# First gated layer on the column layout: 128-byte load runs, the second factor turned, the following norm beside its output

## The reference, cut to what matters

```python
# L0_conv, z = _ln_c(x); i and j are the two positions, c the channel
zn = _layernorm(z, ln_in_w, ln_in_b)
a = sigmoid(zn @ Wga + bga) * (zn @ Wla + bla)
b = sigmoid(zn @ Wgb + bgb) * (zn @ Wlb + blb)
k = einsum('bimc,bmjc->bijc', a, b)            # the only one that contracts a's second with b's first position
out = sigmoid(zn @ Wgo + bgo) * (_layernorm(k, ln_o_w, ln_o_b) @ Wlo + blo)
x = x + out
# L0_ffn: experts choose their top tokens, from the router's logits over all tokens
t = tokens(x);  t = t + L0_ffn(_ln_t(t), ...)
```

## Time and profile before

| | us |
|---|---|
| median of three runs | 665.69 (665.5 to 666.53) |
| the profiled execution | 664.4 |
| its span | 662.6 |
| PE, DVE, ACT, POOL busy in it | 461.7, 424.8, 286.3, 250.3 |

### The profile page before, as it was taken

One profiled execution on the slowest core, in us unless ns is written; L12 is line 12 of the kernel. 1 busy time (PEld: TensorE's weight loads), 2 busy tenths in 40 slices (PEclk: granted clock), 3 DMA queues, 4 the chain that ended last, 5 costly groups with the idle time before them and its releaser, 6 DMA issues.

```text
span 662.6 us, 8339 instructions
## 1 busy us (share of the span) xinstructions
PE 461.7 (70%) x3015; PEld 358.8 (54%) x3015; DVE 424.8 (64%) x829; ACT 286.3 (43%) x658; POOL 250.3 (38%) x310
## 2 busy tenths in 40 slices
PE   2788744799476774798369983798389736738775
PEld 1457642578243653398349972498256625615443
DVE  6796459533958579601954469501958595499996
ACT  2776535601475455565460015566379544000000
POOL 1893554100467158200050003200359376045563
PEclk9999965876689785899859996989579975559999
DMA  6000000000000000000000000000000000001212
GB/s 203 1 1 1 1 1 0 0 1 0 1 0 1 1 0 2 0 1 1 1 0 1 1 2 1 0 1 1 1 0 1 1 1 0 1 0 29 36 30 35
DMA packets 19576, 6.01 MB, mean 9 GB/s; under 512 B 17068, under 2 KB 19244, under 8 KB 19501
## 3 DMA queue, kind: packets, MB, share of 16 engines
q1 hardware_dynamic: 19534, 5.46, 3.6%
HBM read 3.36 MB, written 2.10 MB: 8 GB/s over the span
## 4 chain that ended last, share of the span: by engine, by line
PE 41%; DVE 35%; POOL 10%; issue 8%; ACT 5%; DMA 1%; DVEq 0%; SPq 0%; POOLq 0%
PE psum L1242 6%; DVE stats L279 5%; POOL z L1513 5%; PE psum L1003 4%; DVE ab L647 4%; PE psum L1002 4%; PE psum L506 4%; PE psum L386 4%; PE psum L536 4%; DVE stats L282 3%; DVE z L292 3%; DVE stats L286 2%; PE psum L1385 2%; PE psum L1024 2%; ACT z_t L318 2%
## 5 line engine op out<-in xcount | busy, mean ns | idle before, releaser
L333 POOL TENSOR_TENSOR z<-z,stats 128x496 f32<-128x496 f32 (+1 forms) x64 | 79.2, 1238 | 177.2 <-DVE stats L289 177.2
L386 PE MATMUL psum<-ident,z 128*128 128x128 f32 x256 | 59.2, 377 | 77.8 <-POOL z L333 75.6
L386 PEld LDWEIGHTS psum<-ident,z 128*128 128x128 f32 x256 | 41.1, 192 | 108.0 <-POOL z L333 74.7
L506 PE MATMUL psum<-wp_L,z_t 64*128 64x320 f32 x384 | 65.9, 482 | 11.9 <-DVE tmp L647 6.4
L309 ACT ACTIVATE squares<-z 128x512 f32<-128x512 f32 x64 | 40.3, 630 | 57.5 <-DVE z L292 57.3
L506 PEld LDWEIGHTS psum<-wp_L,z_t 64*128 64x128 f32 x384 | 37.8, 202 | 35.6 <-issue 29.4
L1513 POOL TENSOR_TENSOR z<-gate 128x512 f32<-128x512 f32 x31 | 39.1, 1282 | 30.1 <-DVE gate L1488 30.1
L1095 ACT ACTIVATE ab<-psum,mv 128x128 f32<-128x128 f32 x112 | 41.1, 367 | 19.5 <-PE psum L1003 9.0
L318 ACT ACTIVATE z_t<-psum 128x512 f32<-128x512 f32 x56 | 39.7, 715 | 21.3 <-PE psum L386 21.1
L1003 PE MATMUL psum<-ab,R_vt 128*128 128x128 f32 x224 | 48.5, 300 | 0.0
L1002 PE MATMUL psum<-z_t,wbnt 128*128 128x128 f32 x224 | 46.4, 291 | 0.8 <-DVE wbnt L1148 0.8
(11 more groups left out here) (243 smaller groups left out, 1029.0 us busy)
## 6 DMA issues: line engine op xcount, KB each, us to landing
x_rows<-in_x_dram SPq DMA_DIRECT2D x4, 512.0 KB, 6.9
out_dram<-x_cols SPq DMA_DIRECT2D x32, 64.0 KB, 1.9
par<-in_par_dram SPq DMA_DIRECT2D x1, 644.5 KB
w<-in_w_dram SPq DMA_DIRECT2D x1, 264.0 KB
w<-in_w_dram SPq DMA_DIRECT2D x1, 256.0 KB
mask<-in_mask_dram SPq DMA_DIRECT2D x1, 64.0 KB
row<-in_row_dram SPq DMA_DIRECT2D x1, 3.3 KB
w2l<-in_w2l_dram SPq DMA_DIRECT2D x1, 2.0 KB
```

The lines of the kernel that those rows point to most:

```text
L333: pool.tensor_tensor(Z4[:, r, :, 0:last_c], Z4[:, r, :, 0:last_c], rstd, ALU.mult).then_inc(L.s["z"], 1)
L386: m = pe.transpose(bank(b % 2)[:, k * N:(k + 1) * N], block_of(Z)(4 * b + k), ident[:, :])
L506: m = pe.matmul(bank(slot_bank(s) + h, 2 * 5 * C), ZT[rows, s, :], wp[l][rows, :, :], start=True, stop=True)
```

## The change

L0 moves to the column layout: its source is `XC` and its scratch `XR`. The load writes `XC` from DRAM with the first position inside the partition, so every descriptor moves 32 channels, 128 bytes. Each quarter is 4 DMAs, one for each g, 16 in all in place of 4; the parameters still come after the first quarter. With the second position on the partitions it is `b` that must be turned (`BT`, same storage, same helper, same number of transposes), and the products come out on columns. V0 is gone. F0 takes its chunks straight from L0's last step (`x_chunks(t0)`), its norm is handed over as `after`, and its first logits product waits until L0 has left the PSUM banks (`banks_free`).

```diff
-        X_LOADED = [[(x_in[q * LOADS // Q], 16)] for q in range(Q)]
+        X_LOADED = [[(x_in[q * LOADS // Q], 16 * G)] for q in range(Q)]
-        t0 = stage("L0", "norm weights ones tri", "at_ps at_act at_dve", src=XR, scratch=XC, eps=0, e2=EPS)
-        v0 = stage("V0", "turn_x", src=XR, dst=XC)
+        t0 = stage("L0", "norm weights ones tri", "bt_ps bt_act bt_dve", src=XC, scratch=XR, eps=0, e2=EPS)
-        v0.ready = x_done(t0)
-        f0.ready = [turned(v0)] * Q
+        f0.ready = x_chunks(t0)
+        f0.banks_free = [(t0.s["o_mul"], t0.at["o_mul"] + S // 4)]
...
-                lhs, rhs = AT, ABt[:, 1]
+                lhs, rhs = BT, ABt[:, 0]
-                    turn_pe(pe, L, b, lambda c: ABt[:, 0, c, :], "at_ps", "at_act", "at_dve")
+                    turn_pe(pe, L, b, lambda c: ABt[:, 1, c, :], "bt_ps", "bt_act", "bt_dve")
...
+                    if b == 0:
+                        wait_all(pe, L.banks_free)
                     pe.wait_ge(L.s["zt"], L.at["zt"] + b + 1)
                     m = pe.matmul(bank(2 + r), gw[:, q, :], ZT[:, 4 * b:4 * b + 4, :], start=(q == 0), stop=(q == 1))
...
-            X4, D4 = blocks(XR), x_d.rearrange("i (g s) c -> i g (s c)", g=G)
+            XC4, D4 = blocks(XC), x_d.rearrange("(g s) j c -> j g s c", g=G)
-                f = slice(q * NC // G // LOADS, (q + 1) * NC // G // LOADS)
-                sp.dma_start(XR[:, :].rearrange("p (g f) -> p g f", g=G)[:, :, f], D4[:, :, f]).then_inc(x_in[q], 16)
+                r = slice(q * S // LOADS, (q + 1) * S // LOADS)
+                for g in range(G):
+                    sp.dma_start(XC4[:, g, r, :], D4[:, g, r, :]).then_inc(x_in[q], 16)
...
-            tri_pool(pool, t0, None)
-            ln_pool(pool, f0)
+            tri_pool(pool, t0, f0)
...
-            tri_act(act, t0, None)
-            turn_x_copy(act, v0, 0)
-            ln_act(act, f0)
+            tri_act(act, t0, f0)
...
-            tri_dve(dve, t0, None, {
+            tri_dve(dve, t0, f0, {
-            turn_x_copy(dve, v0, 1)
-            ln_dve(dve, f0)
...
-            turn_x_pe(pe, v0)
```

More of the change, by code:

```diff
@@ L121, in build @@
         AB = sb("ab", [N, 2 * NC])
-        AT = ZT
+        BT = ZT
         GATE = sb("gate", [N, NC])
@@ L524, in tri_pe @@
             if L is t0:
-                lhs, rhs = AT, ABt[:, 1]
+                lhs, rhs = BT, ABt[:, 0]
                 for b in range(C // 4):
-                    turn_pe(pe, L, b, lambda c: ABt[:, 0, c, :], "at_ps", "at_act", "at_dve")
+                    turn_pe(pe, L, b, lambda c: ABt[:, 1, c, :], "bt_ps", "bt_act", "bt_dve")
             for b in range(C // 4):
                 if L is t0:
-                    pe.wait_ge(L.s["at_dve" if b % 2 else "at_act"], L.at["at_dve" if b % 2 else "at_act"] + b // 2 + 1)
+                    pe.wait_ge(L.s["bt_dve" if b % 2 else "bt_act"], L.at["bt_dve" if b % 2 else "bt_act"] + b // 2 + 1)
                 if b >= 4:
@@ L588, in tri_act @@
                 for b in range(0, C // 4, 2):
-                    turn_copy(act, L, b, AT[:, 4 * b:4 * b + 4, :], "at_act", "at_ps")
+                    turn_copy(act, L, b, BT[:, 4 * b:4 * b + 4, :], "bt_act", "bt_ps")
             warm_table(act, ACT.Sqrt)
@@ L657, in tri_dve @@
                 for b in range(1, C // 4, 2):
-                    turn_copy(dve, L, b, AT[:, 4 * b:4 * b + 4, :], "at_dve", "at_ps")
+                    turn_copy(dve, L, b, BT[:, 4 * b:4 * b + 4, :], "bt_dve", "bt_ps")
             for b in range(1, C // 4, 2):
@@ L1559, in _ @@
             out4 = out_d.rearrange("(g s) j c -> j g s c", g=G)
-            XC4 = blocks(XC)
             for b in range(S // 4):
```

## The result

The changed kernel takes 657.49 us in the median of four runs (655.41 to 660.4); the kernel before, 665.61. The ratio is 0.9878, 95% interval 0.9832 to 0.9924: 8.1 us less, where 7.8 were forecast. A second set of six runs of the unchanged text gave 0.9881 (0.9863 to 0.9900). The profiled execution took 659.11 us, so its span is one of the longer ones, and 5.3 us shorter than the span before.

The account below looks back on a forecast made before the run. A chain of waits shared by PE and DVE was taken as the bound, transfers holding 1%. Seam - 9.0 plus load + 1.2 gave - 7.8, from 665.69 to 657.9 us; own range 656 to 660, over the cases 655.5 to 662.5.

Parts of the forecast that it names:

- The seam: Between L0's output and F0's norm: dropping V0 and interleaving the norm gains 8.6 to 9.4 us, taken as 9.0.
- The turned factor: In L0, turning `b` in place of `a`, with the same transposes, copies and product shapes, costs 0.
- The load: At the start, short-packet quarters and four issues bring the parameters 0.4 to 2.0 us later, taken as 1.2, all on the path.
- The rate: Column load of x: packets of 128 bytes take 9.4 to 12.2 ns per engine, taken from the output store's bursts.
- The sign that I had named: At the start, the load's busy slices should show 200 to 220 GB/s.
- A: L0's norm becomes bound by the load at 16 to 22 ns a packet, losing 2 to 7 us; chance 0.14.
- B: The load, from 24 ns a packet, makes the change lose; 671.9 us at 30 ns; chance 0.06.
- Rival C: Behind F0's norm PE's clock could fall to the lower level, adding 4 us, 661.9 in all; chance 0.08.
- my own sign: The prediction is wrong if the stages behind 120 us are longer than before.
- Rival D: At the seam F0's norm still waits for L0's end, so only the turn goes: 7.1 less 1.2, 659.8 us; chance 0.04.

Follow-up runs that it names:

- Experiment 3: Changed kernel with F0's norm again behind L0 on POOL, ACT and DVE, column layout, load and missing V0 kept; 660.36 us (0.9921).
- experiment 1: The changed kernel run again with no edit, against the kernel before; 657.13 us, all runs 656.5 to 659.6.
- experiment 6: Changed kernel with unread PE transposes of the identity filling idle time in the norms of SC and R2; 657.51 us.
- experiment 2: Changed kernel with load runs of 1 KB, still sixteen DMAs, so the layers compute on the turned image; 655.34 us (0.9848).
- experiment 9: Kernel before, row layout, with its load cut into 16 DMAs with runs of 1 KB; 666.61 us (1.0013).
- experiment 10: Changed kernel with every x load DMA doubled into the gates' buffer, ACT waiting for the copies before the first gate; 665.45 us (0.9987).
- experiment 8: Kernel before with parameters issued ahead of x and DVE's first weight step ahead of the norm's first step; 664.96 us (0.9988).
- experiment 5: Changed kernel with the two parameter loads issued by ACT at its start, beside x's first quarter on the sync queue; 657.37 us (0.9870).

## Why the prediction was right, point by point

*The seam, 9.0 us.* Measured: 9.17 and 9.49 us in two profiles. The analogues told it because the interleaved pipeline is the same code on the same tiles; L3's stretch, 39.47 us, was nearer than L1's, as argued: the changed kernel's two are 39.68 and 39.36. Experiment 3 splits it into the turn (7.3) and the interleaving (1.9). The wait `banks_free` sits where R1's did: PE's first router product begins at 102.02, behind the last L675, as in L1. Behind the last root nothing moved (4.54 us before, 113.09 + 0.60 - 109.15 = 4.54 after).

*The turned factor, 0.* From the first L366 to the first L557 the kernel before took 13.75 us and the changed one 69.47 - 55.72 = 13.75.

*The load, 1.2 us.* In size, the parameters came 0.81 us later in the first profile and 1.09, 1.04 and 1.56 later in the three others with this start (experiments 1, 3 and 6), 1.1 in the mean, all against one profile of the kernel before. In mechanism, I had them wait behind 4096 short packets and behind four issues. Experiments 2 and 9, with an eighth of the packets and the same delay, seem to speak against it. The DMA view settles more: the parameters' packets are the only ones of 2 KB and more at the start, 129 in all, so they can be counted apart, as the total less those under 2 KB. Two of these views, before and after, from 0 to 5.5 us:

```profile
DMA packets 643, 1.12 MB, mean 203 GB/s; under 512 B 16, under 2 KB 528, under 8 KB 643
...
DMA packets 4184, 0.65 MB, mean 118 GB/s; under 512 B 4160, under 2 KB 4160, under 8 KB 4184
```

That is 115 of the 129 before and 24 after. The same count, in steps of 0.25 us:

| | first seen by | most by | all 129 by | DVE's first weights |
|---|---|---|---|---|
| before | 4.00 (4) | 5.50 (115) | 6.50 | 7.01 |
| changed | 4.75 (1) | 6.75 (111) | 7.50 | 7.82 |
| experiment 1 | 5.00 (6) | 7.00 (116) | 7.50 | 8.10 |
| experiment 2, 1 KB | 3.75 (3) | 5.75 (113) | 7.75 | 8.28 |
| experiment 9, 1 KB, rows | 3.75 (3) | 5.75 (113) | 7.50 | 8.05 |

In the changed kernel the parameters start some 0.75 to 1 us later, when x's first quarter is through (3952 short packets by 4.75 us, 4118 by 5.00), inside the 4.4 to 5.1 that I had put down, and end as much later. This is the predicted mechanism. Whether the packets or the issue held them is not separated: their issue begins at 3.27 us, and with the 1.15 us that experiment 2 has from issue (2.60) to first packets (3.75) they could have started at 4.4. In the two forms with runs of 1 KB they start no later than before, and 113 are through by 5.75. But the last 16 take until 7.50 or 7.75, while x's next packets pass between them (344 GB/s in all from 5.75 to 7.75 us in experiment 2); before, 124 were through by 5.75 and the last by 6.50. So the cut into four DMAs a quarter has a delay of its own, of about the same size, which I had not foreseen. Why the last packets lag there, no run shows.

*The rate.* The store's rate, with its gaps, was a good stand-in for the load's. Windows of the changed kernel, GB/s in the last column:

```profile
5.00:10.00 5.00, 1.20 (x5) 1.17 (x6) 4.02 (x12) 0.63 (x1) 0.12 (x1) 1.00 1.00 225
10.00:15.00 5.00, 2.44 (x8) 1.71 (x8) 2.67 (x9) 0.94 (x2) 0.00 (x0) 1.00 1.07 169
```

The second is x alone: 169 GB/s, 12.1 ns a packet for each of 16 engines, between the 9.4 and 12.2 drawn from the store's burst and at its slow end. The sign that I had named, 200 to 220 GB/s, was too high: it left the gaps out. It is about half of the 344 GB/s of the 1 KB runs; whether the run length or the pitch in DRAM does that, no run separates. For the same reason the store's rows can't show, as I had read them, that the pitch costs nothing: every store has both. Over all, the last x issue ends at 14.48 us, and chunk 6 is read at 21.31. A and B did not happen, and experiment 10 shows that they were the right thing to fear.

*What was missed* is the time that PE takes inside L0. A delay of 0.81 us at the third chunk became 1.90 from the third projection group on. The PE timelines of before,

```profile
24.98 0.81 PE L506 MATMUL psum<-wp_L,z_t 64*128 64x320 f32 x4
...
30.65 0.81 PE L506 MATMUL psum<-wp_L,z_t 64*128 64x320 f32 x4 [0.69 <-ACT z_t L318]
```

and of the changed kernel:

```profile
25.78 1.44 PE L505 MATMUL psum<-wp_L,z_t 64*128 64x320 f32 x4
...
28.20 0.94 PE L505 MATMUL psum<-wp_L,z_t 64*128 64x320 f32 x4
...
32.55 0.81 PE L505 MATMUL psum<-wp_L,z_t 64*128 64x320 f32 x4 [0.69 <-ACT z_t L317]
```

The second group takes 0.81 us before and 1.44 after: PE's durations fall to those of the high level near 25 us in the one and near 28 in the other, after similar work. How much of that belongs to the change is open. From the third chunk to the first turn of products the profile of the kernel before takes 55.14 us, the shortest of all; the row layout's other two (experiments 8 and 9) take 55.54 and 55.68, nine profiles of the column layout 55.45 to 56.17, and experiment 2's 57.87. Against those two, the first profile's loss is 0.5 us and not 1.0: about half of it is the luck of the one profile that I compared with.

*The sum.* The forecast was - 9.0 + 1.2 = - 7.8, and the medians differ by 8.1 and 8.2. From landmark to landmark experiment 1's profile gives - 9.49 at the seam, + 1.09 at the parameters, + 0.74 inside L0 and + 0.48 behind the seam, - 7.18 in all; the first profile gives - 9.17 + 0.81 + 1.01 + 2.07 = - 5.28. The profiled execution of the kernel before was itself 1.2 us under its median, which makes up for the rest. So the two terms of the forecast were right in size, two small costs were not in it, and that the whole agrees to 0.3 us is luck: the range of 656 to 660 is what the working could claim.

*Rival C* is true of single executions: the first profile gave back 2 us that the second kept, and 1.55 of them are V1's turn at the lower level. By my own sign, stages behind 120 us longer than before, the prediction would have been called wrong from the first profile alone. Over the medians it costs little. That it widens the runs is not shown: the changed kernel's lie from 655.4 to 660.4 and from 656.5 to 659.6, the kernel before's within 1 us in the first set but from 664.0 to 667.1 beside experiment 1. *Rivals A and B* did not happen. *Rival D* is out: the interleaving works and is worth 1.9 us, the value that the working left it.

## What to carry to other kernels

Where the same pipeline already runs interleaved elsewhere in the kernel, its stretch from landmark to landmark prices the new seam to half a microsecond. At a start, order the loads, and the instructions that wait for them, as the chain behind them wants them: experiment 5 brought the parameters early and left DVE waiting for something else. When a transfer is cut into more DMAs, ask again; packets of different size can be counted apart, which tells whose data are late. A profiled execution holds one course of PE's clock, so differences of 2 us behind the changed place need a second profile before they are explained.

## What the runs showed of the hardware

- Loads with runs of 128 bytes reached 169 GB/s in the stretch that held them alone, near the mean of the store's bursts with the same runs (12.2 ns a packet, 168 GB/s); runs of 1 KB reached 344. An issue took 0.83 us each of the last twelve, 0.47 with runs of 1 KB (5.58 us for twelve).
- With runs of 1 KB behind them in the queue, the last 16 of the parameters' 129 packets were through up to 1.75 and 2 us behind the other 113 (experiments 2 and 9); in the changed kernel, with 128-byte runs behind them, the last 18 took 0.75 us.
- A DVE scaling of 16 numbers a partition took 1.21 us beside a POOL sum of 128x512 and ended with it, 0.17 us alone.
- The column of the granted clock says 1.00 in the first 30 us of the kernel before, where PE's turns take 1.11 us and later 0.66 for the same four: at the start the level has to be read from durations.
- Filling PE's idle time with transposes between waits left three turns at 1.12 us, the duration of the low level, over 5 us; the granted clock there was 0.57, against 0.50 without.
